# A fourth key stack in the attention's ring, and three of the eight key splits moved behind the bias additions

## The reference

```python
x = x + tanh(g_xattn[0]) * align(ctx, layernorm(x))          # time warping
x = x + tanh(g_ffn[0]) * quantised_ffn(layernorm(x), ...)    # first feed-forward block
x = x + tanh(g_xattn[1]) * attention(layernorm(x), ctx, ctx, Wq, bq, ..., Wo, bo)
x = x + tanh(g_ffn[1]) * pattern_ffn(layernorm(x), ...)      # three top-k selections
```

```python
k = (key @ Wk.T + bk).reshape(B, Skv, H, Hd).transpose(0, 2, 1, 3)
scores = einsum('bhqd,bhkd->bhqk', q * SCALE, k)
out = einsum('bhqk,bhkd->bhqd', softmax(scores), v).reshape(B, Sq, D) @ Wo.T + bo
```

## Time and profile before

| | us |
|---|---|
| three executions, median | 570.64 |
| the profiled execution | 572.05 |
| its span | 570.3 |
| PE, DVE, ACT busy | 381.9, 389.9, 266.4 |
| POOL busy | 84.8 |
| mean granted TensorE clock | 0.817 of full speed |

### The profile page before, as it was taken

One profiled execution on the slowest core, in us unless ns is written; L12 is line 12 of the kernel. 1 busy time (PEld: TensorE's weight loads), 2 busy tenths in 40 slices (PEclk: granted clock), 3 DMA queues, 4 the chain that ended last, 5 costly groups with the idle time before them and its releaser, 6 DMA issues.

```text
span 570.3 us, 9305 instructions
## 1 busy us (share of the span) xinstructions
PE 381.9 (67%) x2998; PEld 255.8 (45%) x3002; DVE 389.9 (68%) x1644; ACT 266.4 (47%) x684; POOL 84.8 (15%) x215
## 2 busy tenths in 40 slices
PE   2899799812229699777898888899999404403006
PEld 2558586501127455553576666676455201103004
DVE  7643999989983759996876666671454574474773
ACT  3854544622231566245575565877443351452440
POOL 6791000000006063630420000000000000000000
PEclk9998699955558799989888899999999855855556
DMA  9800002377203588430694855501990000000002
GB/s 266 243 1 1 0 2 98 120 142 160 49 1 96 110 135 161 142 97 20 128 157 74 203 82 84 83 1 46 410 371 22 1 0 2 0 1 0 2 1 64
DMA packets 38534, 50.96 MB, mean 89 GB/s; under 512 B 5957, under 2 KB 35030, under 8 KB 37334
## 3 DMA queue, kind: packets, MB, share of 16 engines
q1 hardware_dynamic: 38486, 50.37, 37.1%
HBM read 40.28 MB, written 9.97 MB: 88 GB/s over the span
## 4 chain that ended last, share of the span: by engine, by line
PE 39%; DVE 33%; ACT 13%; DMA 6%; issue 5%; POOL 3%; SPq 1%; DVEq 0%; ACTq 0%; POOLq 0%
PE ps L2166 8%; ACT below L1759 7%; DVE PR L1057 5%; DMA ks<-key_parts 4%; PE ps L2000 4%; PE ps L2105 3%; PE ps L2116 3%; PE ps L2130 3%; DVE R L991 2%; PE ps L1945 2%; DVE prod L1053 2%; PE ps L1861 2%; ACT E L1727 2%; DVE PR L1055 2%; PE ps L2286 2%
## 5 line engine op out<-in xcount | busy, mean ns | idle before, releaser
L1271 DVE TENSOR_REDUCE negm<-ps 112x1 f32<-112x375 f32 x128 | 64.3, 542 | 28.6 <-PE ps L2105 28.2
L1727 ACT ACTIVATE E<-ps 125x448 f32<-125x448 f32 x96 | 49.3, 545 | 28.8 <-PE ps L2116 27.0
L2254 PE MATMUL ps<-cnt,same 128*128 128x7 bf16 (+3 forms) x36 | 6.2, 171 | 71.1 <-ACT below L1759 65.1
L2105 PE MATMUL ps<-ks,qs 96*112 96x375 bf16 x128 | 44.8, 365 | 9.9 <-DMA ks<-key_parts 6.8
L2116 PE MATMUL ps<-qs,ks 99*125 99x112 bf16 x384 | 40.1, 231 | 5.3 <-ACT E L1727 3.4
L2116 PEld LDWEIGHTS ps<-qs,ks 99*125 99x125 bf16 x384 | 35.8, 145 | 13.7 <-ACT E L1727 10.1
L1259 DVE TENSOR_REDUCE acts<-gel 128x4 f32<-128x448 f32 x32 | 19.8, 621 | 30.9 <-ACT gel L1691 30.9
L2254 PEld LDWEIGHTS ps<-cnt,same 128*128 128x128 bf16 (+1 forms) x36 | 4.0, 110 | 73.9 <-issue 73.9
L2130 PE MATMUL ps<-E,v 125*32 125x112 f32 x768 | 31.5, 274 | 0.1
L1691 ACT ACTIVATE gel<-ps 128x448 f32<-128x448 f32 x32 | 17.3, 543 | 29.3 <-PE ps L2166 29.3
L788 POOL CAST kp<-kx 128x750 bf16<-128x750 f32 x8 | 6.5, 812 | 163.2 <-ACT path L1605 125.1
(11 more groups left out here) (372 smaller groups left out, 1014.0 us busy)
## 6 DMA issues: line engine op xcount, KB each, us to landing
ks<-key_parts SPq DMA_DIRECT2D x48, 187.5 KB, 6.7
piwT<-fn_process_input_weights SPq DMA_DIRECT2D x4, 2048.0 KB, 16.9
key_parts<-kp SPq DMA_DIRECT2D x48, 93.8 KB
ctx_again<-in_ctx SPq DMA_DIRECT2D x7, 512.0 KB
keys<-kx SPq DMA_DIRECT2D x16, 187.5 KB, 2.1
kx<-keys SPq DMA_DIRECT2D x8, 375.0 KB, 6.0
ctxP<-in_ctx SPq DMA_DIRECT2D x8, 256.0 KB, 6.5
patT<-in_L_ffn_input_patterns SPq DMA_DIRECT2D x1, 2048.0 KB, 14.3
```

What stands on the lines that cost most here:

```text
L1271: drain(dve.tensor_reduce(negm[:, n:n + 1], bank(nm)[0:S, 0:SC], AX.X, ALU.max, negate=True), nm)
L1727: drain(fn(E[:, (KCH * f + c) % 6, :], bank(nm)[0:KC, 0:4 * S], ACT.Exp), nm)
L2105: fill(mm(bank(nm)[0:S, 0:SC], qs[0:SR, n, S * (u // 4):S * (u // 4) + S], ks[0:SR, u // 4 % 3, n, :], start=True, stop=True), nm)
```

## The change

There is a fourth stack, `ks_last`, in the memory of the float32 queries `qx32` and of part of their split `qp`, both dead once the far queries are stored. Batch b now uses stack b % 4 (batches 3 and 7 the new one). Its ones are written by one more DMA. `load_stack(3)` waits for no product, and `load_stack(b)` for b >= 4 waits for the end of batch b - 4 instead of b - 3. Only the splits of batches 0 to 4 stay where they were; those of 5, 6 and 7 stand behind the bias additions in GpSimd's list. Their stores, and the load of the keys of batch 7, go into SP's loop over the stacks, each store ahead of the stack load of the batch before.

```diff
+EARLY = 5
...
+        ks_last = Region(queries_at).take("ks_last", [128, NH, SC], BF16)
+        assert queries_at + 2 * NH * SC <= rt.at
+
+        def stack(b):
+
+            return ks_last[:, :, :] if b % 4 == 3 else ks[:, b % 4, :, :]
...
-                    sp.dma_start(ks[HD * j:HD * j + HD, b % 3, :, :], key_parts[b, part]).then_inc(stack_loaded[b % 3], 16)
+                    sp.dma_start(stack(b)[HD * j:HD * j + HD], key_parts[b, part]).then_inc(stack_loaded[b % 4], 16)
...
-            for b in range(2, B):
+            for b in range(2, EARLY):
                 store_parts(b)
-                if b + 2 < B:
-                    load_keys(b + 2)
+                load_keys(b + 2)
                 if b == 2:
                     load_stack(2)
...
-            for b in range(3, B):
-                wait_filled(sp, ("scoreT", 4 * b - 9, KCH - 1))
+            sp.dma_start(stack(3)[SR:SR + 3], onesb[0:3, :].unsqueeze(1).broadcast_to([3, NH, SC])
+                         ).then_inc(loaded["ones_last"], 16)
+            load_stack(3)
+            for b in range(4, B):
+                if b + 1 < B:
+                    store_parts(b + 1)
+                    if b + 3 < B:
+                        load_keys(b + 3)
+                wait_filled(sp, ("scoreT", 4 * b - 13, KCH - 1))
                 load_stack(b)
                 if b == 4:
                     sp.wait_ge(x_ready, 2 * B)
...
             wait_drained(pool, ("ffn_up", 0, 1))
-            for b in range(2, B):
+            for b in range(2, EARLY):
                 split_keys(b)
...
                 pool.tensor_tensor(x[:, b, :], x[:, b, :], gbo[:, :], ALU.add).then_inc(bias_added, 1)
+            for b in range(EARLY, B):
+                split_keys(b)
...
-                        pe.wait_ge(stack_loaded[u // 4 % 3], 16 * len(K_PARTS) * (u // 12 + 1))
+                        pe.wait_ge(stack_loaded[u // 4 % 4], 16 * len(K_PARTS) * (u // 16 + 1))
+                    if u == 12:
+                        pe.wait_ge(loaded["ones_last"], 16)
```

More of the change, by code:

```diff
@@ L477, in bankb @@
             return ps[plan[name].banks[0]][:, :].bitcast(BF16)
-        names = ("x",) + tuple(f"ctx{b}" for b in range(B)) + ("again", "ones_k", "attnW", "ffnW", "small", "biasT", "pat", "oiw",
+        names = ("x",) + tuple(f"ctx{b}" for b in range(B)) + ("again", "ones_k", "ones_last", "attnW", "ffnW", "small", "biasT", "pat", "oiw",
                  "opat", "pval", "piw")
@@ L499, in build_program @@
         keys_loaded = [sem(f"keys_loaded{i}") for i in range(2)]
-        stack_loaded = [sem(f"stack_loaded{i}") for i in range(3)]
+        stack_loaded = [sem(f"stack_loaded{i}") for i in range(4)]
         def counter(eng, s):
@@ L618, in _ @@
             for b in range(3):
-                sp.dma_start(ks[SR:SR + 3, b, :, :], onesb[0:3, :].unsqueeze(1).broadcast_to([3, NH, SC])
+                sp.dma_start(stack(b)[SR:SR + 3], onesb[0:3, :].unsqueeze(1).broadcast_to([3, NH, SC])
                              ).then_inc(loaded["ones_k"], 16)
@@ L2104, in scores_for_maximum @@
                 n = 4 * (u % 4) + i
-                fill(mm(bank(nm)[0:S, 0:SC], qs[0:SR, n, S * (u // 4):S * (u // 4) + S], ks[0:SR, u // 4 % 3, n, :],
+                fill(mm(bank(nm)[0:S, 0:SC], qs[0:SR, n, S * (u // 4):S * (u // 4) + S], stack(u // 4)[0:SR, n, :],
                         start=True, stop=True), nm)
@@ L2116, in scores_less_maximum @@
                     ins = mm(bank(nm)[0:KC, S * i:S * i + S],
-                             ks[0:SR + 3, f // 4 % 3, n, KC * c:KC * c + KC],
+                             stack(f // 4)[0:SR + 3, n, KC * c:KC * c + KC],
                              qs[0:SR + 3, n, S * (f // 4):S * (f // 4) + S],
```

## The result

The changed kernel took 568.20 us (median of 20 executions, 563.19 to 571.92), the kernel before 571.66 us in the same session (20 executions, 566.93 to 577.93): a ratio of 0.9934, 95% interval 0.9912 to 0.9955. That is 3.8 us gained, within 2.6 and 5.0, where 10.0 were forecast.

What follows compares the result with a forecast made beforehand. It took late key-stack loads, which stalled TensorE in the attention, and VectorE waiting for GpSimd in the first feed-forward block as the bounds; 4.5 + 5.5 = 10.0 us gained gave 561 us, range 555.5 to 567.5.

Steps and rivals of the forecast that it cites:

- The feed-forward term: First feed-forward block: moving the splits of batches 5 to 7 out frees VectorE from waiting for GpSimd; 4.5 us gained.
- The collision: Attention, step 3: the cut of batch 1's maxima may wait for four GpSimd split instructions, up to 3.3 us more.
- its cover: Attention, steps 7 to 15: the queue hides the cut's wait, so its net cost is zero.
- The attention term: Steps 7 to 23: earlier stack loads remove most stalls and slow clocks; 5.5 us gained.
- Rival 2: Attention gives nothing because stores run at the stack's 139 GB/s, 4.1 us each; 566 us; 24%, worst form included.
- Its worst form: Rival 2 with stacks also served more slowly beside other traffic, 11.1 us each; 569 us; 3 of the 24%.
- One backlog on one queue, so I add up what stands in it: Attention's DMA queue: four slot waits become one backlog, and summed service times tell when each stack is usable.
- SP itself is no limit: SP's issuing in the attention: stores and loads are issued in less time than they are served.
- The service times: Attention's queue: a stack 8.3 us, patT 6.5, a store 2.0, the keys 1.3, the ones 0.3.
- The forecast's own check: TensorE's waits in the attention: none at steps 11, 19 and 23, about 3 us at step 15.
- a sign of being wrong: Attention: forecast wrong if step 15 doesn't wait, steps 11 or 19 do, or VectorE's saving becomes idle time.
- rival 1: Attention: services overlap, so the queue doesn't bind; 9.9 us gained there, 14.4 in all, 556 us; 15%.

Runs made afterwards that it cites:

- experiment 6: Experiment 3 with GpSimd also waiting for the maxima's parts of batch 1 before it splits batches 5 to 7; 564.99 us, ratio 0.9887.
- Experiments 7 and 10: 7: kernel before plus 14 needless transfers after step 23, 581.19 us; 10: changed kernel plus 64 small products long before the attention, 567.22 us.
- experiment 4: Changed kernel with SP waiting for nearly every group of transfers to land before issuing the next; 580.96 us, ratio 1.0143 to the kernel before.
- the second profile: Profile from running the changed kernel again, unaltered; that run's median 566.76 us, ratio 0.9921, the profiled execution 572.09 us.
- experiment 3: Changed kernel with patT issued behind the last stack load instead of batch 4's ("patT last"); 563.19 us, ratio 0.9839; again 564.15 us, 0.9818.
- the paced kernel: Experiment 3 with each stack load released three steps later, when step 4b - 10 ends; 560.00 us, ratio 0.9779; again 557.90 us, 0.9735.

## Why the prediction was wrong

**The feed-forward term was right.** 4.5 us forecast; 4.5 us less on VectorE, 4.0 us at the attention.

**The collision was right, its cover too.** VectorE's timeline of after, the parts of the maxima of batch 1, beside GpSimd's splits 5 and 6 from 281.12 on:

```profile
284.19 0.31 DVE L1321 CAST negp<-negm 112x16 bf16<-112x16 f32 x1
284.53 0.18 DVE L1323 TENSOR_TENSOR negm<-negm,negp 112x16 f32<-112x16 f32 x1
284.74 1.43 DVE L1325 CAST negp<-negm 112x16 bf16<-112x16 f32 x1
286.21 0.72 DVE L1327 TENSOR_TENSOR negp<-negm,negp 112x16 bf16<-112x16 f32 x1
```

Three of the four were stretched; they take 2.74 us from start to end where they took 0.83. GpSimd's timeline has

```profile
283.65 0.81 POOL L806 CAST kp<-kx 128x750 bf16<-128x750 f32 x1
284.54 1.60 POOL L808 TENSOR_TENSOR kp<-kx,kp 128x750 bf16<-128x750 f32 x1
```

so the third operation ends at 286.17, when GpSimd's subtraction has ended at 286.14, and the one that kept its 0.18 us began at 284.53, in the gap between two of GpSimd's. The last operation, 0.72 us, ends at 286.93, as GpSimd's next cast does (286.08 to 286.89). That is the lock for a whole instruction of the Trainium skill, "SBUF — State Buffer", "Who interferes with whom": the trace agrees with it, the exception included. Steps 3 to 4 take 5.9 us instead of 2.9, 3.0 against 3.3 forecast, part of it slow clock (0.50 in 287.0 to 289.4 us). In experiment 6 nothing was won by taking it away.

**The attention term failed, 5.5 us forecast and about nothing found.** By the medians 3.8 less the 4.0 ahead leaves -0.2. Rival 2 had the outcome (566 us, its worst form 569, 24%), but not its first reason: the packets of a store, 43 to 48 ns each, add up to 2.1 to 2.3 us (2.0 forecast), not 4.1, and those of stacks 3 and 4 to 8.0 to 8.6 us (8.3). Its worst form, stacks served more slowly beside other traffic, is in part what happened to stack 4 (below). Three steps of the working failed:
- *"One backlog on one queue, so I add up what stands in it": one item was missing from the sum, TensorE's own code.* I called the engines full and asked only whether a stack would be late. The profile counts each of the 24 fetches on the same 16 engines. By the forecast step 11 comes at 51.7 us after step 0 - 5, without a stall; it came at 59.4 in one profile, 5.45 us of it in two halts, with a clock of 0.78 and 0.79 in 296 to 304 and 304 to 312 us. In the other it came at 53.7, with a halt of 2.14 us and a stack wait of 1.84. The sign stood in the earlier trace rows: the share was already above 1.0, and the change lengthened how long it would be. Experiments 7 and 10 show this cause, and the comparison of all edges that the lateness of the fetch decides each halt; in experiment 4, with hardly any backlog, there are no halts.
- *"SP itself is no limit" was wrong.* 15.59 us of issuing behind patT (16.14 in the second profile) put stack 5 at 318.03. That is 56.2 us after the start of step 0 - 5; before it was 58.8 (327.3), so of the lead of a batch, 12 us, 2.6 were left. In the first profile nothing waited for that stack all the same; in the second step 15 did, for 2.53 us. Moving patT (experiment 3) is worth 5.4 us between ratios 0.9839 and 0.9934, but it takes away bytes and halts with SP's wait, so how much of it is SP's is not shown.
- *The service times were added as if each transfer had the engines to itself.* From the first packet of stack 3 to the last of stack 4 there were to be 20.2 us less the 0.3 of the ones; they were 26.0 and 26.2 us (288.36 to 314.36, and 289.96 to 316.11). The keys' 1,500-byte packets took 64 ns (median) in the feed-forward block and 165 to 200 ns (means) between the stack's, 2.9 and 2.8 us in all for 1.3 forecast. And the engines don't move in step: the first packets of patT ran at 308.56, when stack 4, ahead of it in the queue, had 5.8 us to go; 65 of patT's 256 packets, 3.8 us of the engines' time, ran before stack 4 was through. Two readings of the rows were off besides. By the earlier trace rows patT needs 7.0 us and not 6.5 (2 us at 131 GB/s and 5.0 at 365 make its 2.1 MB). And the stack of batch 3 was not through at 304.1 in the trace before: its last packet ended at 305.89, 0.5 us before the first product and not 2.3, so a stack took 8.4 to 9.2 us from first packet to last. In the paced kernel, where nothing stands behind the stack but a store, stack 4 took 302.60 to 313.50, 10.9 us instead of 14.2. In the second profile step 11 waited for it.

The forecast's own check, "no wait at steps 11, 19 and 23, one of about 3 us at step 15", came out as 2.53 us at step 15 in one profile and none in the other, where the halts had already taken the time. In the one with the wait step 11 waited too, 1.84 us, which the forecast had named as a sign of being wrong. What was forecast for the attention was there to be had: in the profile without halts the paced version gains 9.6 us in it (100.0 against 109.6), near rival 1's 9.9.

**What stays open.** A late fetch decides a halt, but why a fetch is late in one execution and not in another was not found: for the edge behind 3009 the same transfers had been issued in the changed kernel and in experiment 3, and the fetch came 8.4 and 7.7 us late in the one, 3.8 and 4.2 in the other; in the paced one, with stack 4 not yet issued, 9.1 and 6.0. The profile doesn't show when a fetch is asked for. Why pacing beats "patT last", if it does, I read from one profile without halts; the other has two (4.08 and 1.36 us), so whether they are rarer in it is not shown. The 1.3 us that two profiles differ by ahead of 193 us were not looked into.

## What to carry to other kernels

When a change removes waits in front of DMA issues, it turns them into a backlog: list everything that uses the DMA engines in that stretch, the fetch of the engines' own instructions included, and compare how long a new request would stand with how long TensorE runs on one page of code (here 7.0 to 9.3 us, and the packet had to begin 2.5 us before its end). An idle stretch in the middle of a group of like instructions, with "issue" as releaser and at distances of 256 in the instruction count (waits for semaphores counted), is that fetch. The fourth slot with an eager queue gained 3.8 us here; with the big transfer that nobody needs soon put last, and the slot freed early but used late (a paced release), it gained 12.7 and 15.2.

## What the runs showed of the hardware

- A code fetch of TensorE stood 8.4 and 10.1 us behind SP's transfers, and halted TensorE for 3.55 and 1.90 us; behind needless transfers of 17 us, 9.2 us and a halt of 4.84 us. Over 17 halts it went on 2.4 to 3.6 us after the fetch's packet had begun; where it came to the page's end 2.5 us or more after that start, no halt was longer than 0.80 us.
- Behind the halt of 4.84 us the granted clock was 0.53 for 16 us.
- Behind a full queue SP needed 15.59 us to issue six DMAs of 96,000 bytes; with less in front of them 3.94 us.
- A packet of 1,500 bytes took 64 ns (median) ahead of the attention and 165 to 200 ns (means) between packets of 12,000 bytes; one of 750 bytes 40 to 48 ns (means).
- On VectorE a 112x16 cast took 1.43 us beside GpSimd's split, and 0.18 us without.
